# A new order of steps in layers two and three of a four-layer conditioned transformer kernel

## The chip, the cores and the metric

The kernel runs on one core of a Trainium2 chip. The metric is the device time of one execution in microseconds; the kernel before takes 1639.73 us (median of 3 runs, 1638.11 to 1639.75). TensorE is called PE here, its weight loads PEld, VectorE DVE, ScalarE ACT, GpSimd POOL, and SyncE, which issues nearly all the DMAs, SP.

## What is computed

Sixteen sequences of 256 tokens, 256 features each, in float32, go through four residual blocks. The last three have attention with 16 heads of 16 features, and they are the layers 1, 2 and 3 of the kernel:

```python
x = x + low_rank(x, cond_256, cond_64)          # block 0: three small matrices
x = x + block1(x)   # x' = x + attn(rmsnorm(x)); x' + silu(x'' @ gate) * (x'' @ hid) @ out
x = x + block2(x)   # softmax(q k / 4), v, a coherence gate per head, a field term, out projection
x = x + block3(x)   # scores masked, softmax, v, out projection, rms norm, scale and shift
# attention in each: p = softmax(q k^T / sqrt(16));  o = p v;  o @ Wo
```

## The kernel before

**Steps and their order.** The whole work of one sequence (a batch, b = 0 to 15) in one layer is cut into named steps, and each engine runs its part of every step. `SLOT` (lines 37 to 51) gives each step a time in slots relative to its batch, 16 slots to a batch; `LATER` (line 52) shifts single steps on single engines. `plan` and `schedule` (lines 133 to 162) sort all steps of all layers and batches by that time, and each engine's program is written in that order. So the table sets the order alone: the engines wait for each other by semaphores, and a number that changes without passing another step on the same engine changes nothing. Three batches are in work at once. I call the stretch on PE from `probs` 0 of batch b to `probs` 0 of batch b+1 *window b*; in it stand the heads of batch b, the scores of batch b+1, the projections of batch b+2 and the end of batch b-1.

**The steps that matter here**, for head k, with their lines:

- `q`, `k` (PE line 1034, banks of two): projections. ACT copies the result rounded into `qk_hi` (L899 in layer 2, L901 in layer 3), DVE writes the rest into `qk_lo` (L490, L494).
- `stack` 0 to 3 (SP, L670): three DMAs each, which carry `qk_hi`, `qk_hi`, `qk_lo` into `qs` (0, 2) or `ks` (1, 3) for heads 0 to 7 (0, 1) or 8 to 15 (2, 3).
- `smax` k (PE L1099): scores of a head, tokens first; DVE takes the row maxima (L528; with the mask L525 in layer 3) into `rowmax`.
- `neg` u (DVE L535, L537): minus the eight maxima of half u, as a rounded part and a rest, into `negs`.
- `max` u (PE L1107): turns `negs`; DVE copies the bank into `nm` (L542), SP sends it by DMA into two rows of `qs` (L682). From then on the scores come out shifted.
- `probs` k (PE L1116, in layer 3 with the mask's L1114 ahead): shifted scores, keys first; ACT takes the exponential (L922).
- `pv` 0 to 3 (PE L1128): four heads each, and a copy on ACT after 1 and 3 (L926).
- `wo`: output projection (PE L1162); in layer 2 DVE adds the bias into `y` (L580) and POOL adds `y` to the residual (L768).
- `squares` of layer 3: ACT squares and sums the output of `wo` (L938, two instructions), POOL makes the inverse root of it (L788, L790).
- `resid` of layer 3: DVE scales the output of `wo` by that root and the modulation (L615, two instructions), POOL adds the shift (L772) and adds to the residual (L775), SP stores it (L685).

`smax`, `max` and `probs` use the four banks of one ring, in the order in which PE runs them: each waits until the reader of the use four places before is done. The projections and transposes share a ring of two banks.

Of the kernel before, what the change touches and what calls it, by code (L numbers as in the profile page):

```python
# [1267 lines left out]
```

How the kernel before makes its waits and increments, by code:

```python
    def wait_filled(self, eng, *use):  # L98
        eng.wait_ge(self.sem, self.index[use] + 1)
        return self.bank(*use)
# [1 line left out]
    def wait_free(self, pe, *use):  # L102
        u = self.index[use] - len(self.banks)
        if u >= 0:
            event, b, k = self.read[u]
            pe.wait_ge(event.sem, event.at(b, k))
        return self.bank(*use)
# [268 lines left out]
        def start_layers(eng):  # L376
            eng.wait_ge(s_ld0, 16 * (len(loads0) + 2))
            eng.wait_ge(s_ld[1], 16 * len(loads1))
# [11 lines left out]
            def link(a):  # L391
                count[0] += 1
                a.then_inc(s_vch, 1)
                dve.wait_ge(s_vch, count[0])
# [1 line left out]
            def eliminate(name):  # L397
                for j in range(HC - 1):
                    part = slice(j, HC + j + 1)
                    link(dve.stream_shuffle(gj_row[:, part], gj[:, part], mask=[j] * 32))
                    link(dve.reciprocal(gj_c[:, 0:1], gj_row[:, j:j + 1]))
                    link(dve.scalar_tensor_tensor(gj_c[:, 1:2], gj[:, j:j + 1], gj_c[:, 0:1], below[:, j:j + 1], ALU.mult, ALU.mult))
                    link(dve.scalar_tensor_tensor(gj[:, part], gj_row[:, part], gj_c[:, 1:2], gj[:, part], ALU.mult, ALU.add))
                    mark[name, j] = count[0]
                link(dve.tensor_tensor(gj_row[:, 0:HC], gj[:, 0:HC], ident[0:HC, 0:HC], ALU.mult))
                link(dve.tensor_reduce(gj_c[:, 2:3], gj_row[:, 0:HC], AX, ALU.add))
                mark[name] = count[0]
                dve.wait_ge(s_root, "AC".index(name) + 1)
```

## Time and profile before

| | us |
|---|---|
| median of 3 runs | 1639.73 |
| the profiled execution's own time | 1638.78 |
| its span | 1637.0 |
| PE busy | 1542.3 |
| DVE busy | 1044.1 |
| ACT busy | 779.4 |
| POOL busy | 182.1 |

Layer 1 fills the time up to about 780 us with 43.3 us to a batch, layer 2 that from 860 to 1194 us with about 25.6 us, layer 3 that from 1247 to 1606 us with about 25.9 us; between them the layers overlap. A timeline row gives the start, the length and the engine of a run of equal instructions, and in brackets how long the engine had been idle and what ended that. A row of waits gives the total, the number and the longest.

### The profile page before, as it was taken

Reading aid. Unit: us, or ns where it says so; the run is one execution under the profiler, and the core shown is the slowest. Engines: PE = TensorE matmul, PEld = TensorE weight load, DVE = VectorE, ACT = ScalarE, POOL = GpSimd, SP = SyncE. Lnnn points to the kernel's source line nnn. Section 1 sums busy time; section 2 is a strip of 40 time slices with the busy share of each in tenths; the row PEclk is TensorE's granted clock in tenths of the full one; section 3 lists DMA queues with packets and bytes.
Section 4 is the critical chain, followed back from the end, with each engine's and each line's share of the span. In section 5 each row is a group of like instructions: output and inputs, shape, how many; then the busy total and the mean of one; then the engine's idle time right before and its main releaser. Section 6 shows DMA issues by size and latency. Waiting matters only on the chain. (4 is left out here: it accounts for less than half of the span.)

```text
span 1637.0 us, 30596 instructions
## 1 busy us (share of the span) xinstructions
PE 1542.3 (94%) x10971; PEld 1287.6 (79%) x11020; DVE 1044.1 (64%) x3343; ACT 779.4 (48%) x1684; POOL 182.1 (11%) x219
## 2 busy tenths in 40 slices
PE   2569999999999999999999999999999999999997
PEld 1458888888888888888888787887877778777785
DVE  7746555555555555555567767776676776767773
ACT  1335444444444444444445555555555555555554
POOL 7400000000000000000000000000001011110102
PEclk9789999999999999999999999999999999999999
DMA  7074222222222222221235445354453444444340
GB/s 264 7 91 66 44 40 46 46 40 44 47 46 47 47 47 41 37 52 31 40 67 66 69 60 70 51 70 66 60 73 57 76 73 66 85 64 83 69 71 21
DMA packets 99584, 100.09 MB, mean 61 GB/s; under 512 B 11478, under 2 KB 96088, under 8 KB 98794
## 3 DMA queue, kind: packets, MB, share of 16 engines
q1 hardware_dynamic: 99434, 98.14, 36.2%
q8 instruction: 89, 1.46, 0.5%
q14 instruction: 61, 0.50, 0.1%
HBM read 16.83 MB, written 4.19 MB: 13 GB/s over the span
## 5 line engine op out<-in xcount | busy, mean ns | idle before, releaser
L922 ACT ACTIVATE work<-bank 128x512 f32<-128x512 f32 x768 | 453.6, 600 | 244.1 <-PE bank L1116 201.2
L528 DVE TENSOR_REDUCE rowmax<-bank 128x2 f32<-128x512 f32 x512 | 342.9, 687 | 167.7 <-PE bank L1099 163.1
L1116 PE MATMUL bank<-qs,ks 98*128 98x256 f32 x1536 | 401.9, 344 | 0.9 <-DVE rowmax L528 0.6
L1099 PE MATMUL bank<-ks,qs 96*128 96x256 f32 x1536 | 349.8, 310 | 12.7 <-DMA ks<-qk_lo 10.3
L1116 PEld LDWEIGHTS bank<-qs,ks 98*128 98x128 f32 x1536 | 270.2, 192 | 33.2 <-issue 12.4
L1099 PEld LDWEIGHTS bank<-ks,qs 96*128 96x128 f32 x1536 | 243.7, 190 | 39.1 <-DMA ks<-qk_lo 14.7
L525 DVE CUSTOM_DVE_ANT_0 c1t<-bank,big_q 128x256 bf16<-128x256 f32 x512 | 190.4, 421 | 0.7 <-issue 0.7
L1128 PE MATMUL bank<-work,vp 128*32 128x256 f32 x3072 | 185.7, 382 | 0.0
L1128 PEld LDWEIGHTS bank<-work,vp 128*32 128x32 f32 x3072 | 89.9, 109 | 66.1 <-issue 6.0
L948 ACT ACTIVATE work<-bank 128x256 f32<-128x256 f32 x128 | 49.3, 385 | 192.3 <-PE bank L1175 192.3
L1175 PE MATMUL bank<-yt,w_gate 128*128 128x256 f32 x512 | 131.8, 379 | 2.1 <-ACT yt L942 2.1
L1183 PE MATMUL bank<-w_down,work 128*128 128x256 f32 x512 | 131.4, 379 | 0.0
L1175 PE MATMUL bank<-yt,w_hid 128*128 128x256 f32 x512 | 131.4, 379 | 0.0
L926 ACT COPY ot_raw<-bank 128x512 f32<-128x512 f32 x96 | 56.3, 587 | 148.4 <-PE bank L1128 148.4
L1034 PE MATMUL bank<-xt,wqkvo 128*128 128x256 f32 x512 | 120.0, 383 | 2.2 <-ACT xt L886 1.9
L590 DVE SCALAR_TENSOR_TENSOR work<-work,bank 128x256 f32<-128x256 f32 x128 | 53.2, 416 | 96.0 <-ACT work L948 96.0
L1175 PEld LDWEIGHTS bank<-yt,w_hid 128*128 128x128 f32 x512 | 97.2, 190 | 13.4
L1034 PEld LDWEIGHTS bank<-xt,wqkvo 128*128 128x128 f32 x512 | 94.7, 192 | 14.5 <-ACT xt L886 2.7
L1183 PEld LDWEIGHTS bank<-w_down,work 128*128 128x128 f32 x512 | 96.0, 190 | 12.4
L1175 PEld LDWEIGHTS bank<-yt,w_gate 128*128 128x128 f32 x512 | 89.5, 189 | 11.3 <-ACT yt L942 3.0
L494 DVE TENSOR_TENSOR qk_lo<-bank,qk_hi 128x512 fp32r<-128x512 f32 x64 | 43.9, 687 | 81.0 <-ACT qk_hi L901 81.0
L1114 PE MATMUL bank<-big_k,ident_bf 128*128 128x512 bf16 x207 | 80.8, 390 | 0.0
(208 smaller groups left out, 1891.9 us busy)
## 6 DMA issues: line engine op xcount, KB each, us to landing
qs<-qk_hi SPq DMA_DIRECT2D x192, 128.0 KB, 3.9
ks<-qk_hi SPq DMA_DIRECT2D x192, 128.0 KB, 3.8
qs<-qk_lo SPq DMA_DIRECT2D x96, 128.0 KB, 4.3
ks<-qk_lo SPq DMA_DIRECT2D x96, 128.0 KB, 4.3
xres<-in_x_t SPq DMA_DIRECT2D x4, 1024.0 KB, 9.5
x_in<-in_x SPq DMA_DIRECT2D x16, 256.0 KB, 3.2
out<-xres SPq DMA_DIRECT2D x16, 256.0 KB, 2.1
qs<-nm SPq DMA_DIRECT2D x96, 16.0 KB
```

The costliest lines, as they stand in the source:

```text
L525: a = dve.tensor_tensor_reduce(masked[:, k % 2, t, :], bank[:, t * S:(t + 1) * S], big_q[:, t, :], 1.0, 2 * BIG, ALU.add, ALU.max, rowmax[ ...
L528: a = dve.tensor_reduce(rowmax[:, :, k:k + 1], bank[:, :].rearrange("p (t s) -> p t s", t=TC), AX, ALU.max)
L590: dve.scalar_tensor_tensor(act1[:, k % 2, :], th[:, k % 2, :], 1.0, bank[:, 0:S], ALU.add, ALU.mult).then_inc(act1_ok.sem, 1)
L922: act.activation(probs[:, place[n, b, k], :, :], bank[:, :].rearrange("p (c s) -> p c s", c=TC), ACT.Exp, scale=HD ** -0.5)\
L926: act.copy(ot_raw[:, k - 1:k + 1, :], pv_bank[:, :].rearrange("p (g s) -> p g s", g=2)).then_inc(L.o_raw.sem, 1)
L1034: m = pe.matmul(bank[:, c * S:(c + 1) * S], weights[:, i, c * P:(c + 1) * P], acts[:, i, :], start=(i == 0), stop=(i == DC - 1))
L1099: m = pe.matmul(bank[:, t * S:(t + 1) * S], qs[par][0:SCORE_ROWS, k, t * P:(t + 1) * P], ks[par][0:SCORE_ROWS, k, :], start=True, stop=True)
L1114: pe.matmul(bank[:, :], ident_bf[:], big_k[:, :, :].rearrange("p c s -> p (c s)"), start=True, stop=False)
L1116: m = pe.matmul(bank[:, c * S:(c + 1) * S], ks[par][0:SHIFTED_ROWS, k, c * P:(c + 1) * P], qs[par][0:SHIFTED_ROWS, k, :], start=(n != 3), ...
L1128: m = pe.matmul(pv_bank[HW * i:HW * (i + 1), (k % 2) * S:(k % 2 + 1) * S], vp[par][:, c, DC * (j % HALF) + j // HALF, :], probs[:, place[n ...
L1175: m = pe.matmul(bank[:, j * S:(j + 1) * S], wt[:, c, k * P:(k + 1) * P], yt[:, c, :], start=(c == 0), stop=(c == DC - 1))
L1183: m = pe.matmul(acc_bank[:, t * D:(t + 1) * D], hm[:, k % HMBUF, t * P:(t + 1) * P], w_down[:, k, :], start=(k == 0 and t == 0), stop=(k = ...
```

## The change

The table's numbers for layers 2 and 3 change as below; those of layer 1 and `LATER` stay. No operation, no buffer and no wait is changed.

```diff
     2: {
-        "smax": -14.7, "pv": (9.43, 16.76), "neg": (-6.67, 1.15), "max": (-6.24, 2.71), "xT": -26.2, "q": -24.49,
-        "stack": (-23.72, -22.05, -15.9, -14.62), "k": -24.21, "v": -11.32, "tok": 18.5, "load": -30, "coh1": -11.96,
-        "coh2": -10.62, "coh3": -10.31, "vsum": 1.0, "sumv": 19.97, "field": 20.98, "oT": 22.3, "wo": 25.09},
+        "smax": -14.7, "pv": (9.43, 16.53), "neg": (-6.97, 0.53), "max": (-5.84, 2.71), "xT": -26.2, "q": -24.49,
+        "stack": (-23.72, -21.85, -15.9, -14.62), "k": -23.91, "v": -11.32, "tok": 18.5, "load": -30, "coh1": -11.96,
+        "coh2": -10.62, "coh3": -10.31, "vsum": 1.0, "sumv": 19.68, "field": 20.62, "oT": 22.3, "wo": 25.09},
     3: {
-        "smax": -14.03, "pv": (9.2, 15.39), "neg": (-6.23, 1.31), "max": (-6.13, 2.38), "xT": -26.55, "q": -25.22,
-        "stack": (-25.1, -20.12, -15.9, -15.8), "k": -23.34, "v": -11.38, "tok": 18.48, "mod": 13.22, "oT": 20.92, "wo": 22.34,
-        "squares": 22.77, "resid": 24.18},
+        "smax": -14.01, "pv": (9.2, 15.39), "neg": (-6.23, 1.31), "max": (-6.13, 2.38), "xT": -26.55, "q": -25.22,
+        "stack": (-25.1, -20.12, -15.9, -14.57), "k": -23.38, "v": -11.38, "tok": 18.48, "mod": 13.22, "oT": 20.92,
+        "wo": 22.34, "squares": 23.07, "resid": 24.21},
```

What that does to the order, away from the ends of the layers, is seen in four places. The first is PE in the middle of a window of layer 2. L1034 is `q` and `k` (four matmuls each), L1116 `probs`, L1099 `smax`, L1162 `wo`, L1128 two `pv` steps, L1107 `max` 0.

```order
L1034 MATMUL bank<-xt,wqkvo 128x256 x8
L1116 MATMUL bank<-qs,ks 128x256 x2
L1099 MATMUL bank<-ks,qs 128x256 x2
L1116 MATMUL bank<-qs,ks 128x256 x2
L1162 MATMUL bank<-w_gate,ot 128x256 x4
L1099 MATMUL bank<-ks,qs 128x256 x2
L1128 MATMUL bank<-work,vp 32x256 x16
L1107 MATMUL bank<-ident,negs 16x128 x2
L1116 MATMUL bank<-qs,ks 128x256 x2
```

The same place in the changed kernel:

```order
L1034 MATMUL bank<-xt,wqkvo 128x256 x4
L1116 MATMUL bank<-qs,ks 128x256 x2
L1034 MATMUL bank<-xt,wqkvo 128x256 x4
L1099 MATMUL bank<-ks,qs 128x256 x2
L1116 MATMUL bank<-qs,ks 128x256 x2
L1162 MATMUL bank<-w_gate,ot 128x256 x4
L1099 MATMUL bank<-ks,qs 128x256 x2
L1128 MATMUL bank<-work,vp 32x256 x16
L1116 MATMUL bank<-qs,ks 128x256 x2
L1107 MATMUL bank<-ident,negs 16x128 x2
```

`probs` 8 has moved from behind `k` to the place between `q` and `k`, and `max` 0 from before `probs` 10 to behind it.

The second is DVE at the same place, in one piece of the difference. L490 is `q` and `k`, L528 one row maximum, L580 `wo`, L535 and L537 `neg` 0.

```order
-L490 SCALAR_TENSOR_TENSOR qk_lo<-bank,bqk,qk_hi 128x256 x4
-L528 TENSOR_REDUCE rowmax<-bank 128x2
+L490 SCALAR_TENSOR_TENSOR qk_lo<-bank,bqk,qk_hi 128x256 x2
+L528 TENSOR_REDUCE rowmax<-bank 128x2
+L490 SCALAR_TENSOR_TENSOR qk_lo<-bank,bqk,qk_hi 128x256 x2
+L535 TENSOR_SCALAR negs<-rowmax 128x2x8
+L537 SCALAR_TENSOR_TENSOR negs<-rowmax,negs 128x2x8
 L580 TENSOR_TENSOR y<-bank,bout_rows 128x512
 L528 TENSOR_REDUCE rowmax<-bank 128x2
-L535 TENSOR_SCALAR negs<-rowmax 128x2x8
-L537 SCALAR_TENSOR_TENSOR negs<-rowmax,negs 128x2x8
 L542 CAST nm<-bank 16x256
```

`neg` 0 no longer stands behind `wo` and `smax` 8 but ahead of both; `smax` 7 stands between `q` and `k`. (Earlier in the window L569, `field`, has also passed one L528.)

The third is SP in layer 2, again as one place before and after: two DMAs of `stack` 0 and its third, `max` 0 and `stack` 1.

```order
L670 DMA qs<-qk_hi 16x8x256 x2
L670 DMA qs<-qk_lo 16x8x256
L682 DMA qs<-nm 2x8x256
L670 DMA ks<-qk_hi 16x8x256 x2
L670 DMA ks<-qk_lo 16x8x256
```

```order
L670 DMA qs<-qk_hi 16x8x256 x2
L670 DMA qs<-qk_lo 16x8x256
L670 DMA ks<-qk_hi 16x8x256 x2
L670 DMA ks<-qk_lo 16x8x256
L682 DMA qs<-nm 2x8x256
```

The three DMAs of `stack` 1 now stand ahead of that of `max` 0.

The fourth is ACT in layer 3, the only engine whose order changes there. L901 is `q` and `k`, L922 `probs`, L938 `squares`; before:

```order
L922 ACTIVATE work<-bank 128x512 x2
L938 ACTIVATE yn,statb<-bank 128x256 x2
L901 CAST qk_hi<-bank 128x512
L922 ACTIVATE work<-bank 128x512 x2
L901 CAST qk_hi<-bank 128x512
```

and in the changed kernel:

```order
L922 ACTIVATE work<-bank 128x512 x2
L901 CAST qk_hi<-bank 128x512
L922 ACTIVATE work<-bank 128x512
L938 ACTIVATE yn,statb<-bank 128x256 x2
L922 ACTIVATE work<-bank 128x512
L901 CAST qk_hi<-bank 128x512
```

`squares` stood ahead of `q` and stands now behind `q` and `probs` 7. In window 14, which has no `q`, it has passed `probs` 7 alone. POOL's order is the same throughout, and the other new numbers of layer 3 move nothing past anything in its windows.

## Rows read from the trace of the kernel before

**Rows 1.** The page: span, then PE's granted clock (tenths) in 40 slices

```profile
span 1637.0 us, 30596 instructions
...
PEclk9789999999999999999999999999999999999999
```

**Rows 2.** PE, windows 2 to 14, layer 2: xcount | busy, mean ns | idle before, releaser

```profile
L1099 PE MATMUL bank<-ks,qs 96*128 96x256 f32 x418 | 98.7, 318 | 2.8 <-DMA ks<-qk_lo 2.0
...
L1107 PE MATMUL bank<-ident,negs 128*16 128x128 f32 x52 | 10.0, 274 | 4.5 <-DVE negs L537 4.5
```

**Rows 3.** Waits of the weight loads there: total, number, longest, us

```profile
PEld bank L1099 <- DMA ks<-qk_lo: 5.5, 13, 0.8
```

**Rows 4.** Group of `max` on PE, windows 1 to 13 of layer 3

```profile
L1107 PE MATMUL bank<-ident,negs 128*16 128x128 f32 x52 | 10.0, 275 | 9.1 <-DVE negs L537 7.9
```

**Rows 5.** Timeline of SP in window 7 of layer 2

```profile
1010.79 0.65 SPq L682 DMA_DIRECT2D qs<-nm  x1
...
1012.79 0.61 SPq L670 DMA_DIRECT2D ks<-qk_lo  x1
```

**Rows 6.** Timeline of PE, the start of window 8 (`probs` 1, `smax` 0)

```profile
1016.47 0.50 PE L1116 MATMUL bank<-qs,ks 98*128 98x256 f32 x2
1017.06 0.51 PE L1099 MATMUL bank<-ks,qs 96*128 96x256 f32 x2
```

**Rows 7.** Timeline of DVE in window 7 of layer 2

```profile
1005.94 0.88 DVE L490 SCALAR_TENSOR_TENSOR qk_lo<-bank,bqk,qk_hi 128x256 fp32r<-128x256 f32 x2 [0.85 <-ACT qk_hi L899]
...
1008.79 0.87 DVE L535 TENSOR_SCALAR negs<-rowmax 128x16 fp32r<-128x16 f32 x1
...
1010.35 0.41 DVE L542 CAST nm<-bank 16x256 fp32r<-16x256 f32 x1 [0.48 <-PE bank L1107]
1010.84 4.57 DVE L528 TENSOR_REDUCE rowmax<-bank 128x2 f32<-128x512 f32 x7
```

**Rows 8.** Timeline of PE there (two `pv`, `max` 0, `probs` 10, `smax` 9, `probs` 11)

```profile
1007.65 1.93 PE L1128 MATMUL bank<-work,vp 128*32 128x256 f32 x32
1009.93 0.39 PE L1107 MATMUL bank<-ident,negs 128*16 128x128 f32 x2 [0.34 <-DVE negs L537]
1010.07 0.49 PE L1116 MATMUL bank<-qs,ks 98*128 98x256 f32 x2
1010.40 0.40 PE L1099 MATMUL bank<-ks,qs 96*128 96x256 f32 x2
1010.64 0.40 PE L1116 MATMUL bank<-qs,ks 98*128 98x256 f32 x2
```

**Rows 9.** Timeline of ACT in window 7 of layer 3

```profile
1413.80 0.39 ACT L938 ACTIVATE yn<-bank 128x256 f32<-128x256 f32 x1 [0.80 <-PE bank L1162]
...
1416.24 1.30 ACT L922 ACTIVATE work<-bank 128x512 f32<-128x512 f32 x2
```

**Rows 10.** Timeline of POOL there (`squares`, then `resid`)

```profile
1414.99 0.70 POOL L790 TENSOR_TENSOR statb<-statb,half 128x2 f32<-128x2 f32 x1
1419.10 1.29 POOL L772 TENSOR_TENSOR y<-y,x_in 128x512 f32<-128x512 f32 x1 [3.41 <-DVE y L615]
1420.46 1.27 POOL L775 TENSOR_TENSOR xres<-xres,y 128x512 f32<-128x512 f32 x1
```

**Rows 11.** Timeline of DVE there (`resid`, `neg` 0)

```profile
1418.15 0.87 DVE L615 SCALAR_TENSOR_TENSOR y<-bank,statb,x_in 128x256 f32<-128x256 f32 x2
...
1420.55 1.22 DVE L537 SCALAR_TENSOR_TENSOR negs<-rowmax,negs 128x16 fp32r<-128x16 f32 x1
```

**Rows 12.** `neg`, second instruction, all 96: min/median/max ns

```profile
L537 DVE SCALAR_TENSOR_TENSOR negs<-rowmax,negs x96: 174/176/1218, 106.8 to 1608.2; 128x16 fp32r<-128x16 f32 x96
```

**Rows 13.** Timelines of ACT, POOL, DVE, window 14, layer 3 (`probs` 7, root, `resid`)

```profile
1595.22 1.29 ACT L922 ACTIVATE work<-bank 128x512 f32<-128x512 f32 x2
...
1595.68 0.70 POOL L790 TENSOR_TENSOR statb<-statb,half 128x2 f32<-128x2 f32 x1
...
1596.48 0.87 DVE L615 SCALAR_TENSOR_TENSOR y<-bank,statb,x_in 128x256 f32<-128x256 f32 x2
```

## Prediction

> **What bounds the kernel now.** The page comes first: PE is granted its full clock in all slices but two near the start and is the engine that the others follow [rows 1]. So the question in layers 2 and 3 is how long PE stands still, and at which step. I read that from PE's groups of instructions over the steady windows of each layer. In layer 2 two lines have all of it: 2.8 us ahead of L1099, for the DMA of `stack` 1 (`smax` 0 waits for it), and 4.5 us ahead of L1107, `max` 0, which waits for `neg` 0 on DVE [rows 2]. The weight loads, which run ahead of their matmuls, wait 5.5 us for that DMA, once in each of the 13 windows [rows 3]. In layer 3 it is L1107 alone, 9.1 us over 13 windows, two waits in each [rows 4]. In layer 1 nothing of this kind is there and nothing is changed, so a gain or a loss can only come from these 7.3 and 9.1 us and from what is new.
>
> Then come the timelines of single windows, to see what stands behind the two waits. PE alone isn't the whole story: after `max` 0 DVE works through seven row maxima without a pause, 4.57 us or 0.65 us each [rows 7], while PE's own share of a head (one `smax`, one `probs`) is 0.57 us, 1010.07 to 1010.64 [rows 8]. Through the ring of four banks PE goes at DVE's pace there. In that stretch a gain counts only as far as DVE starts its maxima sooner.
>
> **Layer 2, the DMA of `stack` 1.** It now stands behind `max` 0 on SP, whose own DMA can't be issued before `nm` is copied, at 1010.79; so the third DMA of `stack` 1 goes out at 1012.79, though `qk_lo` of `k` has been ready since 1006.82 [rows 5, 7]. In the new order it follows `stack` 0 directly and goes out some 5 us sooner. That is more than the 0.3 to 0.8 us that anything waits for it, so this wait goes away in each of the 13 windows. Its worth: from `probs` 1 to `smax` 0 PE takes 0.59 us in a typical window [rows 6], where from a `probs` to a `smax` that waits for nothing it takes 0.33 [rows 8]. That is 0.26 us in the small windows, of which the visible idle time is 0.09. Over 13 windows, 2.8 us visible and 13 x 0.17 hidden: **5.0 us gained**. The bounds are the 2.8 that PE shows and the 5.5 that the weight loads show. Behind it nothing is late: the `pv` and `probs` ahead of it keep PE at work, and `tok`, next, has its copy by then.
>
> **Layer 2, `neg` 0 and `max` 0.** `neg` 0 now stands behind `smax` 8 and collides with POOL's addition: its first instruction takes 0.87 us and ends at 1009.66 [rows 7]. In the new order it starts when `qk_lo` of `k` is done, at about 1007.2, and is over by 1007.6. PE gets there at 1009.9, so the wait of 0.34 us per window is gone. But how much reaches the time? The two `pv` end and `probs` 10 comes first, at about 1009.5, `max` 0 behind it at 1009.86. That is 0.07 sooner than its 1009.93 of now [rows 8]. DVE's copy follows 0.42 us behind `max` 0 and the first maximum 0.33 behind a copy that nothing holds up: 1010.61, against 1010.84 now [rows 7]. That is 0.23 us. The second maximum may lose a bit again, since PE's `smax` 10 has now `probs` 10 four places before it in the ring, whose exponential on ACT has to wait for the copy behind `pv` 1 and ends at about 1010.75. I take 0.18 us, of 0.34 that were idle: 13 x 0.18 = **2.3 us gained**; bounds 0 and 4.5. The order of `q`, `probs` 8 and `k` moves no PE time, it is the same matmuls on either side, and `field` passes a row maximum while DVE is idle. Both I set at nothing, with 0.1 us a window in the range. At the border of layers 1 and 2 three windows change the same way, but there the down and gate matmuls of layer 1 cover the waits; nothing, with 1 us either way.
>
> **Layer 3, `squares`.** Here nothing on PE moves, and the step that moves is on the path. `squares` starts now as soon as `wo` is done, 1413.80. Its root is ready on POOL at 1415.69, 1.89 us later [rows 9, 10], and DVE begins `resid` at 1418.15 because it has other work until then: a margin of 2.4 us [rows 11]. In the new order ACT does `q` first, for which it has to wait for PE, and then `probs` 7, which starts at 1416.24 [rows 9]. The next instruction can start about 0.48 us behind it, so `squares` starts at 1416.72. With the same 1.89 us the root is there at 1418.61, and as DVE starts `resid` 0.10 us after a root that it waits for (1596.38 and 1596.48) [rows 13], `resid` starts at 1418.71 and not at 1418.15. The margin has turned into a wait of 0.56 us.
>
> What hangs on that is the wait that PE has already. `resid` is followed on DVE without a pause by `smax` 7, `qk_lo` of `k` and `neg` 0, which ends at 1421.77; PE stands at `max` 0 until then, for 0.61 of the window's 0.70 us. `neg` 0 is also tied to POOL: its second instruction takes 176 ns in most cases [rows 12], here 1.22 us, and it ends 0.04 us after POOL's second addition (1420.46 + 1.27) [rows 10, 11]. POOL's additions start from `resid` too. So both ways into `max` 0 shift by the whole 0.56 us, and behind `max` 0 DVE's maxima set the pace again. 13 windows x 0.56 = 7.3 us. In window 14, `squares` passes `probs` 7 alone: it would start 0.48 us behind 1595.22, which is 1.2 us later than now (1596.38 - 1.89 = 1594.49), and `resid` has no margin at all there (it starts 0.10 behind the root) [rows 13]. Another 1.2 us. At the very end of the kernel no `probs` is left to pass. Together **8.5 us lost**; bounds 0, if something else has a margin that I don't see, and 13 x 0.7 + 1.2 = 10.3, if ACT takes `squares` up 0.14 us later than I think.
>
> The Trainium skill's page "SBUF — State Buffer", section "SBUF: two separate sides", says why `neg` 0 would end with POOL's addition: a VectorE instruction in a two-port mode or with two inputs in SBUF, and a GpSimd one, take a shared pair of ports in turn, and the later one is blocked until the other is through. The trace agrees by that rule (0.87 and 1.22 us against 0.17, each ending with an addition on POOL). Without such a rule the pair would have been over at 1420.73, PE would have 0.45 us in hand at `max` 0, and 13 windows of the shift would cost 13 x 0.1 us instead of 7.3.
>
> **The sum.** Gains 5.0 + 2.3 = 7.3, losses 8.5: 1.2 us more. The profiled execution took 1638.78, so 1640.0 for one like it; the median of the runs is 0.95 above that execution, so **1640.9 us** as a median. Less than 0.2% (3.3 us), about what a measurement of this kernel can tell from no change.
>
> **Rivals.** *Layer 2 gains less (slower).* The gain behind the DMA is only what PE shows, 2.8, and that at `max` 0 nothing, because `smax` 10 waits for the exponential of `probs` 10 as long as it now waits for `nm`; it decides if ACT ends `probs` 10 after 1010.85. For it: ACT's copy behind `pv` 1 ends only just before. Then 8.5 - 2.8 = 5.7 more, 1645.4. Chance 0.12.
>
> *The DMA of `nm` gets stuck behind `stack` 1 (slower).* It is issued at 1010.7 and `probs` 0 of the next window loads its weights at about 1013.7; no wait shows, so it lands within 2.9 us now. In the new order up to three DMAs of 128 KB are ahead of it, the last issued at about 1007.7, and one of these took 4.2 us (issued 1012.79, `smax` 0 released at 1017.06) [rows 5, 6]. So they should be through by 1012 and the small one by 1013. From 0.2 us later on every tenth costs 1.3 us over the layer; at 0.5 us it is 6.5 us, 1647.4. Chance 0.10.
>
> *The wait for the root doesn't come, or is absorbed (faster).* If ACT takes `squares` half a microsecond sooner than I think, layer 3 stays as it is and the 7.3 us of layer 2 stand alone: 1632.4. Against it: `probs` 7 can't leave PE sooner, as nothing of PE moves. Chance 0.08.
>
> *`neg` 0 slips in ahead of POOL's second addition (faster).* Its second instruction starts 0.09 us after that addition now [rows 10, 11], in window 14 it got in before it. If a shift in the order of arrival let it in everywhere, `max` 0 would be released at 1421.35 instead of 1421.82, in spite of the later `resid`: 13 x 0.47 = 6 us gained in layer 3, 1639.73 - 7.3 - 6 = 1626. Against it: both start from `resid`, with the same distances. Chance 0.04.
>
> **How the numbers follow.** The forecast's own case has 0.66. Its range is 1637.5 to 1644: 1.5 us for the hidden part of the DMA's wait and the pace behind `max` 0, 1 us for the 0.56, 1 us for the borders. To hold 8 in 10 I go to 1637.0 below and to 1645.5 above, which takes in the first rival and leaves the stuck DMA and the two fast cases outside. Faster by over 0.2% is 0.08 + 0.04 and a little of the forecast's lower edge: 0.14. Slower by over 0.2% is 0.12 + 0.10: 0.22. The rest, 0.64, is no change.
>
> **What would show it.** In the profile after: no wait of L1099 for `ks` in layer 2, and none of L1107 for `neg`; the three DMAs of `stack` 1 directly behind those of `stack` 0; a period of about 25.2 us in layer 2 and 26.4 in layer 3. In layer 3, `squares` about 2.9 us behind the end of `wo`, DVE idle for half a microsecond ahead of L615 with POOL's root as the releaser, L537 still above 1 us, and the idle time of L1107 at 9.1 + 7.3 us over the 13 windows. Wrong would be: a wait of `probs` 0 for the DMA of `nm`, new idle time at `smax` 10 in layer 2, or a group L1107 in layer 3 that has not grown.

## The result and the profile after

| | before | after |
|---|---|---|
| median, us | 1638.92 (4 runs, 1637.86 to 1639.75) | 1625.89 (4 runs, 1623.36 to 1627.33) |
| profiled execution's span, us | 1637.0 | 1624.6 |
| layer 2, windows 2 to 14, us | 334.4 | 325.5 |
| layer 3, windows 1 to 13, us | 337.0 | 329.8 |
| layer 3, window 14, us | 21.93 | 23.11 |
| from `probs` 0 of the last batch to the end, us | 30.9 | 33.1 |

The changed kernel is faster by 13 us: a ratio of 0.9918 with an interval of 0.9902 to 0.9934. I had forecast no change, 1640.9, with a range from 1637.0, so the time lies outside the range, on the side to which I had given 0.14. One of the five executions of e12, the profiled one, took 2243.44 us at a mean granted clock of 0.658, against 0.986 to 0.989 in the other four, and no number below uses it.

The lengths of windows are the distances between the starts of `probs` 0 (L1116) on PE's timeline. They add up: 8.8 us gained in layer 2, 7.2 gained in layer 3, 1.2 lost in window 14 and 2.2 lost behind it make 12.6; window 2 of layer 2 starts 0.2 us later than before, and the difference of the spans is 12.4. Where the length of one window is given below, it is the median of the 13; in layer 3 the first two are up to 0.4 us longer.

The page of the changed kernel (span, then PE's granted clock in 40 slices), beside [rows 1]:

```profile
span 1624.6 us, 30645 instructions
...
PEclk9789999999999999999999999999999999999998
```

**Layer 2.** PE's groups of instructions in the 13 windows 2 to 14, beside [rows 2], and then the waits of the weight loads there, beside [rows 3]:

```profile
L1099 PE MATMUL bank<-ks,qs 96*128 96x256 f32 x418 | 101.0, 323 | 1.0
...
L1107 PE MATMUL bank<-ident,negs 128*16 128x128 f32 x52 | 9.9, 272 | 0.0
```

```profile
PEld bank L1099 <- DVE rowmax L528: 3.9, 21, 0.2
PEld bank L1099 <- ACT work L922: 3.7, 13, 0.3
```

Of the 2.8 and 4.5 us of idle time 1.0 and 0.0 are left, and no weight load waits for a DMA any more. The last line is new: once in each window `smax` 10 waits up to 0.3 us for an exponential on ACT. That is the loss that my working at `max` 0 had allowed for. The wait for the row maxima isn't new, it was 2.0 us in 13 times.

SP's timeline in window 7 shows what took the DMA's wait away (beside [rows 5]):

```profile
1000.50 1.20 SPq L670 DMA_DIRECT2D qs<-qk_hi  x2
...
1003.71 0.62 SPq L670 DMA_DIRECT2D ks<-qk_lo  x1
1006.96 0.65 SPq L682 DMA_DIRECT2D qs<-nm  x1
```

`stack` 1 follows `stack` 0 and is out before the DMA of `nm`. On DVE (beside [rows 7]) both instructions of `neg` 0 are short now and end at 1003.59, long before PE turns to `max` 0, which is behind `probs` 10 and starts at 1006.10 without a wait (beside [rows 8]):

```profile
1003.22 0.17 DVE L535 TENSOR_SCALAR negs<-rowmax 128x16 fp32r<-128x16 f32 x1
1003.41 0.18 DVE L537 SCALAR_TENSOR_TENSOR negs<-rowmax,negs 128x16 fp32r<-128x16 f32 x1
```

```profile
1005.76 0.50 PE L1116 MATMUL bank<-qs,ks 98*128 98x256 f32 x2
1006.10 0.38 PE L1107 MATMUL bank<-ident,negs 128*16 128x128 f32 x2
```

At the start of window 8 the distance from `probs` 1 to `smax` 0 is 0.34 us, where it was 0.59 [rows 6]:

```profile
1012.51 0.50 PE L1116 MATMUL bank<-qs,ks 98*128 98x256 f32 x2
1012.85 0.40 PE L1099 MATMUL bank<-ks,qs 96*128 96x256 f32 x2
```

**Layer 3.** The windows got shorter, from 25.88 to 25.33 us, where I had expected 26.4. PE's group of `max` in windows 1 to 13 has 1.6 us of idle time left of 9.1 [rows 4]:

```profile
L1107 PE MATMUL bank<-ident,negs 128*16 128x128 f32 x52 | 10.0, 275 | 1.6
```

The timelines of ACT, POOL and DVE in window 7, beside [rows 9 to 11]; the L1116 of `probs` 0, from which this window is counted, starts at 1391.07 and that of before at 1403.08:

```profile
1403.51 0.58 ACT L901 CAST qk_hi<-bank 128x512 fp32r<-128x512 f32 x1 [2.53 <-PE bank L1034]
1404.22 0.60 ACT L922 ACTIVATE work<-bank 128x512 f32<-128x512 f32 x1
1404.72 0.38 ACT L938 ACTIVATE yn<-bank 128x256 f32<-128x256 f32 x1
```

```profile
1405.90 0.70 POOL L790 TENSOR_TENSOR statb<-statb,half 128x2 f32<-128x2 f32 x1
1407.65 1.28 POOL L772 TENSOR_TENSOR y<-y,x_in 128x512 f32<-128x512 f32 x1 [1.06 <-DVE y L615]
1409.01 1.31 POOL L775 TENSOR_TENSOR xres<-xres,y 128x512 f32<-128x512 f32 x1
```

```profile
1406.70 0.88 DVE L615 SCALAR_TENSOR_TENSOR y<-bank,statb,x_in 128x256 f32<-128x256 f32 x2 [0.48 <-issue]
1407.50 0.42 DVE L525 CUSTOM_DVE_ANT_0 c1t<-bank,big_q 128x256 bf16<-128x256 f32 x1
...
1408.79 0.18 DVE L535 TENSOR_SCALAR negs<-rowmax 128x16 fp32r<-128x16 f32 x1
1409.00 0.17 DVE L537 SCALAR_TENSOR_TENSOR negs<-rowmax,negs 128x16 fp32r<-128x16 f32 x1
```

Up to `resid` all is as forecast: `squares` behind `probs` 7, POOL's root done at 1406.60, DVE idle for 0.48 us until 0.10 us after it. From the start of the window `resid` (L615) stands at 15.63 us instead of 15.07, which is the forecast 0.56 us later. But L537 takes 0.17 us instead of 1.22. It starts at 1409.00, and POOL's second addition (L775) at 1409.01. Before, the addition was first, at 1420.46, and L537 second, at 1420.55. `neg` 0 has slipped in ahead of the addition, which was the rival to which I had given 0.04. The whole trace says the same, beside [rows 12]:

```profile
L537 DVE SCALAR_TENSOR_TENSOR negs<-rowmax,negs x96: 174/176/177, 108.7 to 1593.5; 128x16 fp32r<-128x16 f32 x96
```

### The profile page after: what moved, and what is told of

The parts are those of the page before. It is cut to its first block and busy times, and to the rows that moved or that the text cites. A ratio compares the mean times of both kernels' runs of the same rounds, so it can differ in the third digit from the quotient of the medians.

```text
span 1624.6 us, 30645 instructions
## 1 busy us (share of the span) xinstructions
PE 1543.2 (95%) x11020; PEld 1289.0 (79%) x11020; DVE 1021.2 (63%) x3343; ACT 773.1 (48%) x1684; POOL 182.5 (11%) x219
## 5 line engine op out<-in xcount | busy, mean ns | idle before, releaser
L922 ACT ACTIVATE work<-bank 128x512 f32<-128x512 f32 x768 | 452.8, 600 | 230.9 <-PE bank L1116 192.1
L528 DVE TENSOR_REDUCE rowmax<-bank 128x2 f32<-128x512 f32 x512 | 343.0, 687 | 155.6 <-PE bank L1099 151.2
L1116 PE MATMUL bank<-qs,ks 98*128 98x256 f32 x1536 | 400.5, 343 | 1.2 <-DMA qs<-nm 0.9
L1099 PE MATMUL bank<-ks,qs 96*128 96x256 f32 x1536 | 353.8, 313 | 9.5 <-DMA ks<-qk_lo 6.7
L1116 PEld LDWEIGHTS bank<-qs,ks 98*128 98x128 f32 x1536 | 270.6, 192 | 37.3 <-issue 17.7
L1099 PEld LDWEIGHTS bank<-ks,qs 96*128 96x128 f32 x1536 | 245.2, 190 | 38.1 <-DMA ks<-qk_lo 7.5
L525 DVE CUSTOM_DVE_ANT_0 c1t<-bank,big_q 128x256 bf16<-128x256 f32 x512 | 190.4, 421 | 0.7 <-issue 0.7
L1128 PE MATMUL bank<-work,vp 128*32 128x256 f32 x3072 | 185.7, 382 | 0.0
L1128 PEld LDWEIGHTS bank<-work,vp 128*32 128x32 f32 x3072 | 89.9, 109 | 65.9 <-issue 5.6
L1034 PE MATMUL bank<-xt,wqkvo 128*128 128x256 f32 x512 | 123.9, 386 | 2.4 <-ACT xt L886 1.9
L1183 PEld LDWEIGHTS bank<-w_down,work 128*128 128x128 f32 x512 | 96.0, 190 | 12.4
L1034 PEld LDWEIGHTS bank<-xt,wqkvo 128*128 128x128 f32 x512 | 94.4, 193 | 14.4 <-ACT xt L886 2.7
L1114 PE MATMUL bank<-big_k,ident_bf 128*128 128x512 bf16 x256 | 100.0, 391 | 0.0
```

The source lines that it names most:

```text
L525: a = dve.tensor_tensor_reduce(masked[:, k % 2, t, :], bank[:, t * S:(t + 1) * S], big_q[:, t, :], 1.0, 2 * BIG, ALU.add, ALU.max, rowmax[ ...
L528: a = dve.tensor_reduce(rowmax[:, :, k:k + 1], bank[:, :].rearrange("p (t s) -> p t s", t=TC), AX, ALU.max)
L922: act.activation(probs[:, place[n, b, k], :, :], bank[:, :].rearrange("p (c s) -> p c s", c=TC), ACT.Exp, scale=HD ** -0.5)\
L1034: m = pe.matmul(bank[:, c * S:(c + 1) * S], weights[:, i, c * P:(c + 1) * P], acts[:, i, :], start=(i == 0), stop=(i == DC - 1))
L1099: m = pe.matmul(bank[:, t * S:(t + 1) * S], qs[par][0:SCORE_ROWS, k, t * P:(t + 1) * P], ks[par][0:SCORE_ROWS, k, :], start=True, stop=True)
L1114: pe.matmul(bank[:, :], ident_bf[:], big_k[:, :, :].rearrange("p c s -> p (c s)"), start=True, stop=False)
```

## The experiments

Ratios are to the kernel before on the same chip, with the interval in brackets. Its median was 1638.33, 1638.10, 1639.34 and 1638.67 us in the four groups of runs (`e1` to `e4`, `e5` to `e8`, `e9` to `e12`, `e13` and `e14`).

### Which part of the table does it

**e1**: the kernel before, with `squares` of layer 3 moved alone.

```diff
-        "squares": 22.77, "resid": 24.18},
+        "squares": 23.07, "resid": 24.18},
```

> The kernel before with one number changed, squares of layer 3 from 22.77 to 23.07: squares behind q and probs 7 on ACT, layer 2 as before. Theory of the slip: resid comes 0.6 us later and so do both additions on POOL, but DVE reaches neg 0 only 0.5 us later, so the second instruction of neg 0 starts just before the second addition and isn't held up; max 0 of layer 3 waits 0.04 instead of 0.61 us, windows 1 to 13 are 0.55 us shorter, window 14 is 1.2 us longer: 6 us faster, 1633. Rival, the gain of layer 3 needs the new order of layer 2 (or the other new numbers of layer 3): no gain here, or 8.5 us slower as I predicted, 1647.

Measured: 1633.57 us, ratio 0.997 (0.9958 to 0.9982). The windows of layer 3 are 25.33 us long and window 14 is 23.11, as in the changed kernel. PE's group of `max` in windows 1 to 13 of layer 3:

```profile
L1107 PE MATMUL bank<-ident,negs 128*16 128x128 f32 x52 | 10.0, 275 | 1.7
```

This single number makes the whole difference in layer 3, with both its signs.

**e2**: the kernel before, with the changed kernel's numbers for layer 2 alone.

```diff
-        "smax": -14.7, "pv": (9.43, 16.76), "neg": (-6.67, 1.15), "max": (-6.24, 2.71), "xT": -26.2, "q": -24.49,
-        "stack": (-23.72, -22.05, -15.9, -14.62), "k": -24.21, "v": -11.32, "tok": 18.5, "load": -30, "coh1": -11.96,
...
+        "smax": -14.7, "pv": (9.43, 16.53), "neg": (-6.97, 0.53), "max": (-5.84, 2.71), "xT": -26.2, "q": -24.49,
+        "stack": (-23.72, -21.85, -15.9, -14.62), "k": -23.91, "v": -11.32, "tok": 18.5, "load": -30, "coh1": -11.96,
...
```

> The kernel before with the new numbers of layer 2 alone, layer 3 as before. Both theories of layer 3 expect layer 3 at 25.88 us per window. Layer 2: windows 2 to 14 together 8.8 us shorter as in the changed kernel, 1630. Rival, part of the gain of layer 2 comes from somewhere else (the start, the border): then 1631 to 1635.

Measured: 1631.16 us, ratio 0.9953 (0.9936 to 0.9969). Windows 2 to 14 of layer 2 take 325.5 us together, as in the changed kernel, and those of layer 3 are 25.88 us long, as before. The two layers don't act on each other here, and their parts can be looked at one by one.

### Layer 3: is it the order of `neg` 0 and POOL's addition?

**e3**: the changed kernel, with one copy more on DVE at `smax` 7 of layer 3. It should put `neg` 0 behind the addition again and leave the rest.

```diff
-        tick = sb("tick", [1, 2])
+        tick = sb("tick", [1, 2]); pad = sb("pad", [P, 64])
...
-                            dve.memset(tick[:, k % 2:k % 2 + 1], 0.0)
+                            dve.memset(tick[:, k % 2:k % 2 + 1], 0.0); k != HALF - 1 or dve.tensor_copy(pad[:], bank[:, 0:64])
```

> The changed kernel with one small instruction more on DVE in smax 7 of layer 3, a copy of 128x64 from the bank to a new tile, some 0.1 to 0.2 us, behind resid and ahead of neg 0. Theory of the slip: neg 0 comes too late by 0.1 us, its second instruction is held up until POOL's second addition ends, 1.1 us; L537 is back above 1 us and max 0 waits 1.1 us more in 13 windows: 15 us slower than the changed kernel, 1641. Rival, the order of arrival at the ports plays no part: only the 0.15 us themselves, at most 2 us slower, 1628.

Measured: 1637.88 us, ratio 0.9999 (0.999 to 1.0008), 12 us above the changed kernel for 16 copies of 0.22 us, 3.5 us in all. I had expected 15. Windows 1 to 13 of layer 3 are 14.1 us longer together than in the changed kernel. One is 26.43 us long, which is the length I had forecast for the changed kernel. Window 7 on POOL and on DVE, and PE's group of `max`:

```profile
1414.68 1.26 POOL L775 TENSOR_TENSOR xres<-xres,y 128x512 f32<-128x512 f32 x1
```

```profile
1414.78 1.19 DVE L537 SCALAR_TENSOR_TENSOR negs<-rowmax,negs 128x16 fp32r<-128x16 f32 x1
```

```profile
L1107 PE MATMUL bank<-ident,negs 128*16 128x128 f32 x52 | 10.0, 275 | 16.3 <-DVE negs L537 15.1
```

L537 arrives 0.10 us after the addition instead of 0.01 before it, takes 1.19 us, and PE's idle time goes from 1.6 to 16.3 us. I had named 9.1 + 7.3 = 16.4. So the forecast was right for the order of arrival that it took for granted.

**e4**: the kernel before, with no step moved; POOL's second addition waits for `neg` 0.

```diff
-                        pool.wait_ge(mod_sum.sem, mod_sum.at(b, 3))
+                        pool.wait_ge(mod_sum.sem, mod_sum.at(b, 3)); b + 2 >= NBATCH or pool.wait_ge(L.negs.sem, L.negs.at(b + 2, 2))
```

> The kernel before, where POOL's second addition of resid in layer 3 waits in addition until neg 0 of the batch two further is done; the order of all engines is that of before. Theory of the slip: L537 takes 0.18 us, neg 0 is over at 0.5 us before PE gets to max 0, the wait of 0.61 us is gone in windows 1 to 13: 13 x 0.6 = 8 us faster, 1631. Rival, neg 0 is slow for a reason of DVE's own (what stands ahead of it): L537 stays at 1.2 us and the time at 1639.

Measured: 1631.54 us, ratio 0.9956 (0.9941 to 0.9971); the windows of layer 3 are 25.21 us long. Its group of `max`:

```profile
L1107 PE MATMUL bank<-ident,negs 128*16 128x128 f32 x52 | 10.0, 274 | 1.1
```

With `squares` where it was, and only the order of these two instructions turned, layer 3 gains 0.67 us a window. The moved `squares` itself costs the 0.12 us between 25.21 and 25.33, and the 1.2 us of window 14.

**e7**: the kernel before, with POOL's second addition replaced by a fill, which reads nothing. The kernel leaves out the last residual sum, so it is there for its times alone.

```diff
-                        pool.tensor_tensor(xres[:, b, :, :], xres[:, b, :, :], y[:], ALU.add).then_inc(L.x_new.sem, 1)
+                        pool.memset(y[:], 0.0).then_inc(L.x_new.sem, 1)
```

> The kernel before, with POOL's second addition of resid in layer 3 replaced by filling y with zeros, so the last residual sum is left out; it writes as much and reads nothing. If what holds up the second instruction of neg 0 is an instruction on POOL that reads SBUF (the Trainium skill, SBUF, State Buffer, section SBUF: two separate sides, says a two-input VectorE instruction loses only against such a one): L537 0.18 us in all windows, the wait of 0.61 us gone, 8 us faster, 1631. If any instruction of POOL on SBUF holds it up: L537 takes as long as the fill lasts, the gain is between 0 and 8 us by its length.

Measured: 1629.34 us, ratio 0.9937 (0.9913 to 0.9961); windows of 25.21 us. Window 7 on POOL and on DVE:

```profile
1416.59 0.54 POOL L775 MEMSET y<- 128x512 f32 x1
```

```profile
1416.70 0.18 DVE L537 SCALAR_TENSOR_TENSOR negs<-rowmax,negs 128x16 fp32r<-128x16 f32 x1
```

L537 starts 0.11 us into the fill and takes 0.18 us. It ends 0.25 us before the fill does, so it isn't POOL's being at work that holds it. The Trainium skill's page "SBUF — State Buffer", section "SBUF: two separate sides", says that a VectorE instruction with two inputs in SBUF contends only against a GpSimd one that reads SBUF, and that whichever starts first holds the shared ports for its whole length. The traces agree on both: 0.18 us beside a fill, 0.17 us when 0.01 us ahead of an addition, 1.19 to 1.22 when 0.09 to 0.10 us behind one. For POOL the trace shows less of it: the addition that L537 precedes takes 1.31 us, where those of before and of e3 take 1.26 to 1.27.

### Can layer 3 keep the gain and lose the cost of `squares`?

**e5**: the changed kernel with `squares` back, and POOL's first addition waiting for `neg` 0 (so that the second one comes later too).

```diff
-        "wo": 22.34, "squares": 23.07, "resid": 24.21},
+        "wo": 22.34, "squares": 22.77, "resid": 24.21},
...
-                        pool.wait_ge(mod_sum.sem, mod_sum.at(b, 2))
+                        pool.wait_ge(mod_sum.sem, mod_sum.at(b, 2)); b + 2 >= NBATCH or pool.wait_ge(L.negs.sem, L.negs.at(b + 2, 2))
```

> Layer 2 as in the changed kernel, squares of layer 3 where it was before, and POOL starts both additions of resid only when neg 0 of the batch two further is done. Theory of the slip: neg 0 is never held up, windows 1 to 13 of layer 3 take 25.2 us as with one addition behind it, window 14 loses its 0.48 us of wait: against the changed kernel 13 x 0.12 + 1.2 + 0.4 = 3.2 us faster, 1623. Rival, the additions, now up to 1 us later, hold up what comes behind them (the copy of the modulation, the store ahead of the DMA of nm on SP): as slow as the changed kernel or slower, 1626 or more.

Measured: 1635.85 us, ratio 0.9982 (0.9972 to 0.9991), some 10 us above the changed kernel. L537 is short everywhere (177 ns at most), as wanted. PE's group of `max` isn't the bound any more; this line of PE's waits in layer 3 is:

```profile
PE bank L1099 <- DMA ks<-qk_lo: 13.2, 13, 2.1
```

SP's timeline shows why:

```profile
1393.94 0.38 SPq L685 DMA_DIRECT2D out<-xres  x1
1394.37 0.65 SPq L682 DMA_DIRECT2D qs<-nm  x1
1395.12 1.20 SPq L670 DMA_DIRECT2D ks<-qk_hi  x2
```

The store of the result (L685) waits on SP for POOL's second addition, which ends at 1393.92 now. The DMA of `nm` and `stack` 1 stand behind it on the same queue, though they don't need it. The rival that I had written down for this run was right, my own expectation was not. Part of the cost is the clock's: windows 3 and 5 take 28.46 and 28.77 us, where most take 25.7, and there the mean granted clock is 0.93 over 1290 to 1315 and over 1340 to 1365 us, behind waits of 1.80 and 2.09 us on PE. A wait of 2.03 us in window 10 had no such dip behind it.

**e6**: the same aim by order alone. `resid` goes behind `neg` 0 on DVE, and its store behind the DMA of `nm` on SP.

```diff
-        "wo": 22.34, "squares": 23.07, "resid": 24.21},
+        "wo": 22.34, "squares": 22.77, "resid": 24.21},
...
-LATER = {"vector": {..., "squares": 0.41}, ..., "sync": {"wo": 0.39}}
+LATER = {"vector": {..., "squares": 0.41, "resid": 1.6}, ..., "sync": {"wo": 0.39, "resid": 2.0}}
```

> The same aim by the order alone: layer 2 as in the changed kernel, squares where it was before, resid of layer 3 1.6 slots later on DVE (behind neg 0) and 2 slots later on SP (behind the DMA of max 0), no wait added. Theory of the slip: POOL's additions begin after neg 0, so L535 and L537 are short everywhere and max 0 waits for nothing; 1623 as the kernel with the two waits. Rival, resid now stands between neg 0 and the copy of max 0 on DVE, and delays the seven maxima behind it: 0.1 to 0.4 us more per window, 1625 to 1628.

Measured: 1639.34 us, ratio 1.0001 (0.9988 to 1.0014). A miss, and for a reason I hadn't seen. PE's longest group of waits in layer 3, and SP's timeline:

```profile
PE bank L1099 <- DMA ks<-qk_lo: 13.9, 13, 2.2
```

```profile
1391.72 0.65 SPq L682 DMA_DIRECT2D qs<-nm  x1
1394.01 0.38 SPq L685 DMA_DIRECT2D out<-xres  x1
1394.49 1.20 SPq L670 DMA_DIRECT2D ks<-qk_hi  x2
```

The DMA of `nm` is free of the store, but `stack` 1 still isn't, and goes out 2.1 us after `nm`'s end.

**e10**: as e6, with `stack` 1 of layer 3 moved ahead of `max` 0 on SP and the store behind all of them.

```diff
-        "stack": (-25.1, -20.12, -15.9, -14.57), "k": -23.38, "v": -11.38, "tok": 18.48, "mod": 13.22, "oT": 20.92,
-        "wo": 22.34, "squares": 23.07, "resid": 24.21},
+        "stack": (-25.1, -22.2, -15.9, -14.57), "k": -23.38, "v": -11.38, "tok": 18.48, "mod": 13.22, "oT": 20.92,
+        "wo": 22.34, "squares": 22.77, "resid": 24.21},
...
-LATER = {"vector": {..., "squares": 0.41}, ..., "sync": {"wo": 0.39}}
+LATER = {"vector": {..., "squares": 0.41, "resid": 1.6}, ..., "sync": {"wo": 0.39, "resid": 4.0}}
```

> The kernel with resid behind neg 0, but on SP in layer 3 now in the order stack 1, max 0, store. If the new waits of smax 0 with resid behind neg 0 came from the store standing ahead of stack 1 (it waits for POOL), they are gone: no wait of L1099 for ks, windows of 25.1 to 25.2 us, 1622 to 1624. Rival, the waits came from the later additions in another way (the copy of the modulation, resid between neg 0 and the copy of max 0): windows above 25.5 us, 1626 or more.

**e11**: the changed kernel with `squares` back and the wait of e4.

```diff
-        "wo": 22.34, "squares": 23.07, "resid": 24.21},
+        "wo": 22.34, "squares": 22.77, "resid": 24.21},
...
-                        pool.wait_ge(mod_sum.sem, mod_sum.at(b, 3))
+                        pool.wait_ge(mod_sum.sem, mod_sum.at(b, 3)); b + 2 >= NBATCH or pool.wait_ge(L.negs.sem, L.negs.at(b + 2, 2))
```

> Layer 2 as in the changed kernel, squares of layer 3 where it was before, and only POOL's second addition behind neg 0. The store then comes at most 0.3 us later than before, not 1 to 2 us as with both additions, and stack 1 behind it in time: windows 1 to 13 of layer 3 at 25.2 us without a wait of smax 0, window 14 at 21.9: 0.12 x 13 + 1.2 = 2.8 us faster than the changed kernel, 1623. Rival, a late store costs here too: a wait of L1099 for ks in layer 3, 1626 or more.

**e12**: the changed kernel once more, beside these two on the same chip.

> The changed kernel itself, as the measure for the two that follow: 1625.9, between 1624 and 1628.

Measured: e10 1620.45 us, ratio 0.9885 (0.9872 to 0.9899); e11 1620.76, ratio 0.9891 (0.9878 to 0.9905); e12 1624.4 (the median of four), ratio 0.991 (0.9897 to 0.9924). The windows of layer 3 are 25.21 us long in e10 and e11, window 14 takes 21.39 in e10 and 21.94 in e11, where the changed kernel has 25.33 and 23.11. Both are some 4 us below the changed kernel. In e10 the only wait of PE for data that is left in layer 3 is one of 0.2 us, for a row maximum.

e10 and e6 differ in nothing but the order on SP, so e6 had failed at the queue. With `stack` 1 out of the store's way, the same idea works; e11 gets there by holding up only the second addition, which delays the store less than e5 does.

### Layer 2: which move is worth what?

**e8** and **e9**: the kernel before with `stack` 1 of layer 2 moved alone, and with `neg` 0 moved alone.

```diff
-        "stack": (-23.72, -22.05, -15.9, -14.62), "k": -24.21, "v": -11.32, "tok": 18.5, "load": -30, "coh1": -11.96,
+        "stack": (-23.72, -22.3, -15.9, -14.62), "k": -24.21, "v": -11.32, "tok": 18.5, "load": -30, "coh1": -11.96,
```

> The kernel before with one number changed, the second of stack of layer 2 from -22.05 to -22.3: on SP the three DMAs of stack 1 stand ahead of that of max 0, nothing else moves. Theory: the wait for ks at smax 0 goes, with its hidden part 0.36 us in most windows, 5.9 us over 13: 1632.7; the wait for neg 0, 0.34 us, stays. Rival, the DMA of nm behind stack 1 comes late and probs 0 waits: gain below 5 us, with a wait of L1116 for nm in the trace.

```diff
-        "smax": -14.7, "pv": (9.43, 16.76), "neg": (-6.67, 1.15), "max": (-6.24, 2.71), "xT": -26.2, "q": -24.49,
+        "smax": -14.7, "pv": (9.43, 16.76), "neg": (-6.97, 1.15), "max": (-6.24, 2.71), "xT": -26.2, "q": -24.49,
```

> The kernel before with neg 0 of layer 2 alone moved ahead of wo and smax 8 on DVE (-6.67 to -6.97). max 0 no longer waits 0.34 us. Theory, DVE sets the pace behind max 0: the same 0.34 us come back only in part if the copy of max 0 starts sooner by as much; here max 0 stands right behind pv 1 and goes 0.34 us sooner, so 0.3 us per window, 13 x 0.3 = 4 us faster, 1634. Rival, smax 9 on DVE is held by PE, gain at most half of it, 1636 to 1637.

Measured: e8 1632.06 us, ratio 0.996 (0.9946 to 0.9973); e9 1632.36 us, ratio 0.996 (0.9945 to 0.9975). PE's two groups in layer 2, windows 2 to 14, of e8 and then of e9:

```profile
L1099 PE MATMUL bank<-ks,qs 96*128 96x256 f32 x418 | 97.5, 315 | 0.0
L1107 PE MATMUL bank<-ident,negs 128*16 128x128 f32 x52 | 10.0, 274 | 4.5 <-DVE negs L537 4.5
```

```profile
L1099 PE MATMUL bank<-ks,qs 96*128 96x256 f32 x418 | 98.8, 318 | 2.8 <-DMA ks<-qk_lo 2.0
L1107 PE MATMUL bank<-ident,negs 128*16 128x128 f32 x52 | 10.0, 274 | 0.0
```

Each move takes away its own wait and leaves the other one as it was. e9's gain is larger than I had expected: a window goes from 25.60 to 25.19 us, 0.41 us instead of 0.3.

**e13**: both moves of one number, and nothing else. **e14**: the same, with what e10 does in layer 3 (`squares` stays where the kernel before has it).

```diff
-        "smax": -14.7, "pv": (9.43, 16.76), "neg": (-6.67, 1.15), "max": (-6.24, 2.71), "xT": -26.2, "q": -24.49,
-        "stack": (-23.72, -22.05, -15.9, -14.62), "k": -24.21, "v": -11.32, "tok": 18.5, "load": -30, "coh1": -11.96,
+        "smax": -14.7, "pv": (9.43, 16.76), "neg": (-6.97, 1.15), "max": (-6.24, 2.71), "xT": -26.2, "q": -24.49,
+        "stack": (-23.72, -22.3, -15.9, -14.62), "k": -24.21, "v": -11.32, "tok": 18.5, "load": -30, "coh1": -11.96,
```

> The kernel before with two numbers of layer 2 changed: stack 1 ahead of max 0 on SP and neg 0 ahead of wo and smax 8 on DVE, but probs 8, k, probs 10 and max 0 on PE where they were. Alone they gave 0.37 and 0.43 us a window. Theory, max 0 behind probs 10 costs what is missing in the changed kernel (there 0.57 together): windows 2 to 14 at 24.8 us, 10.5 us faster than before, 1628.5. Rival, the two gains overlap: 25.03 us as in the changed kernel, 1630.5.

e14 has besides:

```diff
-        "stack": (-25.1, -20.12, -15.9, -15.8), "k": -23.34, "v": -11.38, "tok": 18.48, "mod": 13.22, "oT": 20.92, "wo": 22.34,
+        "stack": (-25.1, -22.2, -15.9, -15.8), "k": -23.34, "v": -11.38, "tok": 18.48, "mod": 13.22, "oT": 20.92, "wo": 22.34,
...
-LATER = {"vector": {..., "squares": 0.41}, ..., "sync": {"wo": 0.39}}
+LATER = {"vector": {..., "squares": 0.41, "resid": 1.6}, ..., "sync": {"wo": 0.39, "resid": 4.0}}
```

> These two numbers of layer 2 and the order of layer 3 with resid behind neg 0 and stack 1, max 0, store on SP. The two layers don't touch each other away from their border, so the gains add up: 10.5 us in layer 2 and 9.3 in layer 3, 1619. If the gains of layer 2 overlap: 1620.5, as the best so far.

Measured: e13 1628.46 us, ratio 0.994 (0.9927 to 0.9952); e14 1616.58 us (1615.80 to 1619.32), ratio 0.9863 (0.9849 to 0.9878). The 13 windows of layer 2 take:

| | us | against before | idle at `smax` 0 | idle at `max` 0 |
|---|---|---|---|---|
| before | 334.4 | | yes | yes |
| e8, `stack` 1 alone | 328.1 | -6.3 | no | yes |
| e9, `neg` 0 alone | 329.0 | -5.3 | yes | no |
| e13, both | 322.9 | -11.5 | no | no |
| the changed kernel | 325.5 | -8.8 | no | no |

The two gains add up (6.3 + 5.3 = 11.6), and what the changed kernel moves besides costs 2.6 us, 0.2 in each window. PE's two groups in e13 have no idle time at all, where the changed kernel has 1.0 us at L1099. The weight loads of L1099 still wait for row maxima in e13 (2.9 us in 19 times, against 3.9 in 21), but never for an exponential:

```profile
L1099 PE MATMUL bank<-ks,qs 96*128 96x256 f32 x418 | 97.5, 315 | 0.0
```

e13 keeps `max` 0 ahead of `probs` 10 and `k` ahead of `probs` 8 on PE, and on DVE it keeps `smax` 7 behind `q` and `k`, and `field` behind the row maximum that it passes in the changed kernel. Which of these the 0.2 us belong to was not tried apart. The wait for ACT's exponential at `smax` 10, which only the changed kernel has, speaks for `max` 0 behind `probs` 10.

e14 beats both kernels: 22 us below the kernel before and 8 (e12) to 9 below the changed one. I had expected 1619, and it took 1616.58.

## Why the prediction was wrong

**What bounds the kernel**: right for what was gained, which all came from the two waits of PE in layer 2 and from `max` 0 in layer 3. Against it stand the 2.6 us of the other moves in layer 2, window 14 and the tail.

**Layer 2, the DMA of `stack` 1**: right, sized a little small. 5.0 us were forecast, e8 has 6.3. Small windows gained 0.37 us instead of the 0.26 I read from the distance between `probs` 1 and `smax` 0. `smax` 0 itself has got shorter too (0.51 to 0.40 us at its start in window 8), which I hadn't counted. That the DMA of `nm` might get stuck behind `stack` 1 didn't happen.

**Layer 2, `neg` 0 and `max` 0**: right. Counted from the start of the two `pv` in window 7 (1007.65 before, 1003.89 in the changed kernel), `max` 0 comes 0.07 us sooner, as forecast, and the first maximum 0.22 us sooner, against 0.23. 2.3 us were forecast; the changed kernel's 8.8 less the 6.3 of e8 leave 2.5. What I hadn't seen is how much the new place of `max` 0 throws away: alone the earlier `neg` 0 is worth 5.3 us (e9), more than my upper bound of 4.5, and the other moves take 2.6 of it back. The loss at `smax` 10 that I had deducted is there, and with it the "new idle time at `smax` 10" that I had named as a sign of being wrong. It cost little: layer 2 as a whole was forecast at 7.3 and measured at 8.8, so the rival by which it gains less didn't come true.

**Layer 3, `squares` up to `resid`**: right. ACT, POOL's root and DVE's idle time stand where they were forecast, and `resid` is 0.56 us later, as forecast. Window 14 lost 1.18 us, against 1.2. And e3, with the order of arrival that the forecast took for granted, has the forecast's windows (26.43 us) and its idle time (16.3 against 16.4).

**The step that failed** is "both ways into `max` 0 shift by the whole 0.56 us", with its reason, "both start from `resid`, with the same distances". The way by POOL did shift as a whole: L772 stands 0.95 us and L775 2.31 us behind the start of `resid` in either kernel. The way by DVE didn't: L537 stands 2.40 us behind it before and 2.30 after. The 0.10 us are between `resid` and the first instruction of `smax` 7 (L525), which follows 0.80 us behind it and no longer 0.91. Before, a small fill of DVE's (L522) stood between them [rows 11]:

```profile
1419.00 0.06 DVE L522 MEMSET tick<- 1x1 f32 x1
1419.06 0.42 DVE L525 CUSTOM_DVE_ANT_0 c1t<-bank,big_q 128x256 bf16<-128x256 f32 x1
```

In the changed kernel L525 starts at 1407.50, before `resid` has ended, and the fill runs beside it. Why wasn't tested. The pause of 0.48 us ahead of `resid` gives PE time to have `smax` 7 ready, which would do it: its matmuls end 0.72 us behind the start of `resid` before, and 0.17 behind it in the changed kernel. The traces fit this but don't prove it. The trace of before had the shorter distance in it too, and I hadn't looked: in window 14, the one window where `resid` already came behind a pause for its root, `smax` 7 is done before `resid` starts, and L525 follows `resid` by 0.80 us there.

So L537 went from 0.09 us behind the start of the addition to 0.01 ahead of it. What that is worth had been written down in the rival: 0.47 us a window from a release at `max` 0 that comes earlier "in spite of the later `resid`". It was 0.55, and 7.2 us over 13 windows instead of 6. That L1107's idle time in layer 3 had not grown was also a sign of being wrong that I had named. I had gone by a margin of 0.09 us between distances that I had read where `resid` follows without a pause, and one of them changed by 0.10 once it came behind one; and I had put 0.04 on that. The effect behind it was a step of over a microsecond in length, and I had seen it in the rows. With a threshold so near, the case on the other side should have had a chance of about its own size, and the range both ends: 1626 and 1641.

**The other rivals.** The trace shows neither a root that isn't waited for nor an `nm` that gets stuck.

**The tail**: 2.2 us were lost behind the last `probs` 0 in the profiled execution, of which my sum had nothing; the last section has it.

## What to carry to other kernels

Where two engines share something that the first to come holds for its whole instruction, look up by how much the arrivals lie apart, before summing. If that is less than the uncertainty of the shift, both orders are cases. An order fixed by a wait or by the order of steps (e4, e10) is better than one that holds by 10 ns, even where something else keeps those 10 ns steady, as here (next section). And read such distances in every window of the trace, also in the odd one at the end: it may be the one that already runs as the change will. And when a step is moved on an engine, look at the stores of its result on the queue: an in-order queue hands a late store's wait to loads that have nothing to do with it (e5, e6).

## What the runs showed of the hardware

**A tenth of a microsecond decides 1.1 us a window.** L537 takes 0.17 us when it starts 0.01 us ahead of POOL's addition and 1.22 us when it starts 0.09 us behind it. In e3, where L537 comes 0.12 us later than in the changed kernel, a window goes from 25.33 to 26.43 us.

**Why a lead of 0.01 us holds.** It is 0.01 us in each of the windows 1 to 14 of the changed kernel and of e1, and in window 14 of the kernel before. DVE and POOL in that window of before (`neg` 0, then the two additions):

```profile
1598.09 0.65 DVE L535 TENSOR_SCALAR negs<-rowmax 128x16 fp32r<-128x16 f32 x1
1598.78 0.17 DVE L537 SCALAR_TENSOR_TENSOR negs<-rowmax,negs 128x16 fp32r<-128x16 f32 x1
```

```profile
1597.44 1.27 POOL L772 TENSOR_TENSOR y<-y,x_in 128x512 f32<-128x512 f32 x1 [1.05 <-DVE y L615]
1598.79 1.30 POOL L775 TENSOR_TENSOR xres<-xres,y 128x512 f32<-128x512 f32 x1
```

The first addition (L772) ends at 1598.71. L535, which started 0.62 us ahead of that end and takes 0.65 us instead of about 0.17, ends 0.03 us behind it; L537 starts 0.07 behind it and the second addition 0.08. In windows 1 to 13 of the changed kernel L535 starts only 0.14 us ahead of the end of L772, and the three distances are the same. So the end of the first addition sets both starts, and the lead doesn't grow if DVE comes still sooner, up to the 0.62 us seen here. It is lost if DVE comes later: in window 7 of before L535 starts 0.03 us ahead of that end, takes its usual 0.16 us, and L537 starts 0.17 behind it:

```profile
1420.36 0.16 DVE L535 TENSOR_SCALAR negs<-rowmax 128x16 fp32r<-128x16 f32 x1
```

As L537 starts 0.19 to 0.20 us behind an L535 that nothing holds, L535 has to start some 0.12 us ahead of the end to win; with 0.14 the changed kernel has about 0.02 us to spare. That is an estimate from these rows.

**The clock at the end.** In the last batch PE idles three times, while `oT`, the normalization of its tokens and `wo` follow on each other, first for 0.71 us ahead of L1144, in both kernels. The other two pauses on PE's timeline, in the changed kernel and then in the one before:

```profile
1611.11 1.12 PE L1050 MATMUL bank<-ident,on 128*128 128x128 f32 x4 [1.37 <-DVE on L561]
1612.78 3.75 PE L1162 MATMUL bank<-w_hid,ot 128*128 128x256 f32 x8 [0.55 <-ACT ot L930]
```

```profile
1625.74 0.65 PE L1050 MATMUL bank<-ident,on 128*128 128x128 f32 x4 [1.37 <-DVE on L561]
1626.95 1.97 PE L1162 MATMUL bank<-w_hid,ot 128*128 128x256 f32 x8 [0.55 <-ACT ot L930]
```

And the stretch of `wo` in the changed kernel, then in the one before (busy time of PE, PEld, DVE, ACT and POOL with counts, then PE's granted clock):

```profile
1612.70:1616.60 3.90, 3.75 (x8) 2.52 (x8) 0.00 (x0) 0.24 (x2) 0.00 (x0) 0.50 0.00 0
```

```profile
1626.90:1629.00 2.10, 1.97 (x8) 1.44 (x8) 0.00 (x0) 0.23 (x2) 0.00 (x0) 1.00 0.00 0
```

The same eight matmuls take 3.75 us at a granted clock of 0.50 (1.2 GHz) and 1.97 at 1.00 (2.4 GHz), behind the same pauses of 1.37 and 0.55 us. The four matmuls of L1050 between the two pauses take 1.12 and 0.65 us. The table doesn't decide which of the two it is: the stretch from the last `probs` 0 to the end is 30.9 us in the profiles of before, e4, e5 and e9, and 31.7 to 33.1 in the others, and e5 (30.9) and e11 (33.1) have the same table. It also differs between executions of one kernel: the fastest of the changed kernel, 1623.36 us, has a mean granted clock of 0.990, and the other three, 1625.40 to 1627.33, have 0.986. So up to 2.3 us of a difference between two single profiles may come from there, which is why the verdicts above rest on windows and on medians. What decides the clock here stays open.
